# Row maximum before the rotary work in the first two steps of a unit of the attention network

## The reference

```
q = l2norm(q) * qs;  k = l2norm(k) * ksc                    # 16 heads of 64
q = q * cos * scale + rotate_half(q) * sin * scale          # rotation; k the same with 1/scale
sim = einsum(q, k in a window) * 8, masked
attn = softmax(sim, -1);  out = attn @ v;  x = out @ Wo + x
x = (a * gelu(gate)) @ W2 + x                               # gated layer behind a layernorm
```

## Time and profile before

| | |
|---|---|
| three runs, median (lowest to highest) | 6375.76 us (6371.46 to 6377.16) |
| the profiled execution: its time | 6374.81 us |
| its span, first to last instruction | 6373.0 us |
| mean granted TensorE clock, share of full speed | 0.931 |
| busy: TensorE, VectorE, ScalarE, GpSimd | 87%, 66%, 59%, 41% |

### The profile page before, as it was taken

The page is one execution under the profiler, slowest core; times in us unless marked ns, Lnnn a source line. Parts: engine busy times, 40 slices in busy tenths (PEclk is TensorE's granted clock), DMA queues, the critical chain, the costliest instruction groups (busy, mean ns, idle before and its releaser), DMA issues. The chain is left out here.

```text
span 6373.0 us, 104346 instructions
## 1 busy us (share of the span) xinstructions
PE 5519.4 (87%) x31072; PEld 3054.5 (48%) x31072; DVE 4211.3 (66%) x6918; ACT 3758.3 (59%) x11805; POOL 2607.4 (41%) x2014
## 2 busy tenths in 40 slices
PE   6888877777768999899998999899998999899997
PEld 3333333223225555555555555555555555555553
DVE  5666665333337777777777777777777777777775
ACT  3444443232226767667766776667666667667775
POOL 2122211000005555555554555555555555555553
PEclk9989988677679999999999999999999999999998
DMA  1000000000012222222222222222222222222222
GB/s 39 0 0 0 0 0 20 0 0 0 0 50 54 48 47 52 52 51 48 48 57 51 48 47 49 53 55 48 49 51 52 51 48 48 57 52 48 49 47 67
DMA packets 160228, 244.68 MB, mean 38 GB/s; under 512 B 51280, under 2 KB 51280, under 8 KB 158928
## 3 DMA queue, kind: packets, MB, share of 16 engines
q1 hardware_dynamic: 159696, 238.34, 15.2%
HBM read 30.52 MB, written 6.29 MB: 6 GB/s over the span
## 5 line engine op out<-in xcount | busy, mean ns | idle before, releaser
L323 POOL TENSOR_TENSOR c_Pb<-c_Pb,c_rs 96x512 f32<-96x512 f32 (+1 forms) x960 | 998.2, 1040 | 1459.4 <-DVE c_rs L715 1459.3
L385 ACT ACTIVATE c_Pb<-c_S,c_nb 96x128 f32<-96x128 f32 (+1 forms) x3840 | 1348.1, 359 | 159.9 <-DVE c_nb L706 158.5
L722 DVE COPY c_PTs<-c_S 128x384 f32<-128x384 f32 (+1 forms) x960 | 558.4, 582 | 623.9 <-PE c_S L506 622.8
L706 DVE TENSOR_REDUCE c_nb<-c_S 96x4 f32<-96x512 f32 (+1 forms) x960 | 657.1, 684 | 401.0 <-PE c_S L496 400.8
L335 POOL TENSOR_TENSOR c_rot<-c_tAB 128x1024 f32<-128x1024 f32 x384 | 910.1, 2370 | 0.8 <-DVE c_tAB L685 0.8
L396 ACT ACTIVATE c_OT<-c_PO 128x192 f32<-128x192 f32 (+1 forms) x960 | 324.4, 338 | 767.9 <-PE c_PO L520 767.4
L385 ACT ACTIVATION_READ_ACCUMULATOR c_Pb<-c_S,c_nb 96x1 f32 (+1 forms) x3840 | 757.7, 197 | 0.0
L329 POOL TENSOR_TENSOR c_sqs<-c_sq 128x512 f32<-128x512 f32 x384 | 488.0, 1271 | 610.4 <-ACT c_sq L363 610.4
L496 PE MATMUL c_S<-c_QK 64*96 64x128 f32 (+1 forms) x7680 | 666.4, 292 | 0.0
L506 PEld LDWEIGHTS c_S<-c,c_Pb 96*128 96x128 f32 (+1 forms) x3840 | 434.0, 142 | 368.0 <-issue 212.5
L520 PE MATMUL c_PO<-c_PTs,c_V 128*64 128x96 f32 (+1 forms) x7680 | 555.8, 266 | 20.1 <-issue 19.5
(11 more groups left out here) (267 smaller groups left out, 10879.5 us busy)
## 6 DMA issues: line engine op xcount, KB each, us to landing
c_QK<-c_F SPq DMA_DIRECT2D x3072, 64.0 KB, 2.0
c_stage<-in_w_heads SPq DMA_DIRECT2D x36, 256.0 KB, 3.0
a_W<-in_w_level SPq DMA_DIRECT2D x1, 3335.5 KB, 11.0
c_WT<-in_w_tails SPq DMA_DIRECT2D x6, 537.5 KB, 5.4
b_W<-in_w_level SPq DMA_DIRECT2D x1, 3133.0 KB, 10.0
c_WT<-in_w_tails SPq DMA_DIRECT2D x6, 512.0 KB, 4.2
x<-in_x SPq DMA_DIRECT2D x1, 2048.0 KB, 7.5
x_kept<-x SPq DMA_DIRECT2D x1, 2048.0 KB, 6.3
```

What stands on the lines that cost most here:

```text
L323: nc.gpsimd.tensor_tensor(p, p, r, ALU.mult).then_inc(*p_ready.up())
L385: e = nc.scalar.activation(Pb[0:m, n % 3, i, :], S[0:m, 2 * (n % 2) + r, c * SPAN_K:(c + 1) * SPAN_K], ACT.Exp, bias=nb[0:m, n % 2, i:i + ...
L706: nc.vector.tensor_reduce(nb[0:m, n % 2].rearrange("p (b c) -> p b c", b=2), S[0:m, b:b + 2, 0:2 * SPAN_K].rearrange("p b (c k) -> p b c k ...
L722: nc.vector.tensor_copy(PTs[:, n % 2].rearrange("p (b c) q -> p b c q", b=2)[:, :, :, 0:m], S[:, b:b + 2, 2 * SPAN_K:].rearrange("p b (c q ...
```

## The change

In VectorE's `step`, four lines move from ahead of `row_max` to behind it. In steps with t = 0, `finish` of the q job now comes behind the row maximum, and in steps with t = 1, `products` of half 1 of the k job does. Nothing is added or removed, and the other engines' lists are the same.

```
@@ VectorE's step
-                    if t == 0 and tk:
-                        finish(jk - 1, tk)
-                    if t == 1 and tk:
-                        products(jk, 1, tk)
                     if n == 2 and now:
                         v_copy(1, 0, PA, now)
...
                     if now:
                         row_max(n, now)
+                    if t == 0 and tk:
+                        finish(jk - 1, tk)
+                    if t == 1 and tk:
+                        products(jk, 1, tk)
                     if t == 0 and tk:
                         products(jk, 0, tk)
```

## The result

| | before | changed |
|---|---|---|
| runs of this comparison, median (lowest to highest) | 6373.86 us (6371.46 to 6377.16), 4 runs | 6538.38 us (6524.08 to 6539.84), 4 runs |
| the profiled execution: time, span | 6374.81, 6373.0 us | 6524.08, 6522.3 us |

The change makes the kernel slower by 2.5%: the ratio is 1.0250, with a 95% interval from 1.0235 to 1.0264. The forecast was 6562, in a range from 6495 to 6620. The profiled execution is the shortest of the four; the other three lie at 6537 to 6540.

The account below looks back on a forecast made before the run. TensorE was taken as the bound, waiting for `finish`: 2.97 us per turn times 48 turns gives 143 us, plus 43 us for clock falls, on 6374.8 us: 6561, or 6562 against the median, range 6495 to 6620.

Parts of the forecast that it names:

- Step 0: First t = 0 step: the projection waiting for `finish` starts 0.65 us later, 0.85 together with step 2's 0.2.
- the 0.2 of step 2: In step 2 the later `products` lets TensorE's projection start at 3943.92 instead of 3943.73, 0.2 us later.
- Step 5: At t = 0 the projection starts 1.38 us later, waiting for `finish`; 0.43 is absorbed, leaving 0.95.
- the 0.1 of step 7: In step 7 the later `products` costs 0.1 us, by the same sum as in step 2.
- moves by the same 1.38: Behind step 5's projection on TensorE, the transpose, copy of probabilities and scores of step 6 each move by 1.38 us.
- Step 10: At t = 0 the projection moves from 3980.18 to 3981.68, by 1.50 us; 0.43 is absorbed, leaving 1.07.
- Step 15: The gated layer's matmuls stand ahead of the projection on TensorE, so the later `finish` costs nothing.
- the gaps and what surrounds them are nearest to those of step 13: New gaps in steps 5 and 10 bring clock falls at step 13's share, 20/42: 43 us for 96 gaps.
- Rival 1: The dependency costs as forecast, but TensorE's clock does not fall in the new gaps: 6518 us, chance 0.26.
- Rival 4: The row maximum is on the chain setting the end; 0.6 us earlier shortens each unit: 115 us faster, 6260, chance 0.05.
- the gain side is empty: Exponentials of steps 5 and 15 start 0.3 and 0.6 us earlier, but TensorE's following work queues behind the projection: no gain.
- Rival 2: The clock falls nearly each time in the new gaps and the delays of `rotate` show: 6609 us, chance 0.08.

Follow-up runs that it names:

- t0_only: Kernel before, with only `finish` (t = 0) moved behind the row maximum and `products` left ahead: 6503.03 us against 6376.35, ratio 1.0199.
- half_finish: Changed kernel, with `finish` computing only 256 of the 512 tokens: 6445.04 us against 6377.4 for the kernel before, ratio 1.0107.
- last_unit_only: Kernel before, with both moves made only in steps 15 and 16: 6386.31 us against 6376.35, ratio 1.0017.
- t1_only: Kernel before, with only `products` of half 1 (t = 1) moved behind the row maximum: 6356.8 us against 6376.35, ratio 0.9967.
- late_proj: Changed kernel, with TensorE's projection of half 1 moved to just ahead of the next step's scores: 6517.62 us, ratio 1.0222 to the kernel before.
- before_split_first: Kernel before, with the weight split ahead of `products` of half 1 in steps 1, 6, 16 of layer-change turns: 6353.58 us against 6377.12, ratio 0.9963.
- after_split_first: Changed kernel, with the weight split ahead of `products` of half 1 in steps 1, 6, 16 of layer-change turns: 6500.65 us, 1.0195 of the kernel before.
- step11_only: Kernel before, with `products` of half 1 behind the row maximum only in step 11, not in layer-change turns: 6335.15 us against 6377.12, ratio 0.9936.
- both_gains: Kernel before, with step 11's `products` behind the row maximum and the weight split first in layer-change turns: 6320.28 us against 6377.4, ratio 0.9911.
- fill_gap: Changed kernel, with TensorE computing the values of steps 3 and 8 three times: 6513.55 us against 6377.12 for the kernel before, ratio 1.0221.

## Why the prediction was right, and where its terms were off

**The mechanism: right.** TensorE's projection waits for `finish`, 1.44 us in steps 5 and 10 as worked out, 0.39 in step 0 (worked out: projection at 3938.99, where the gap comes to 0.38), and nothing in step 15. `t0_only` alone gives the turn of 91.6 us, and `half_finish` moves the wait with the length of `finish`. The idle time ahead of L472 is absorbed as said.

**The ordinary turn: 2.97 forecast, 2.5 measured.** The shifts of the row maxima within a turn show where the difference is. Step 0: 0.85 forecast, 0.65 measured; the 0.2 of step 2 found idle time of the scores behind it, which waited for the copy anyway. Step 5: 1.05 forecast with the 0.1 of step 7, about 0.75 measured; the step that failed is "moves by the same 1.38". Before, the copy of the probabilities was queued on VectorE behind `products` until 3959.99, so scores of step 6 had a delay of their own which the new one covers. Now the copy waits 0.25 us for the transpose. Of the 0.3 this is 0.18: from the start of the projection to that of the mask of step 6 it is 3960.59 - 3958.40 = 2.19 us before and 3937.84 - 3935.83 = 2.01 now.

```profile
3960.59 0.42 PE L491 MATMUL c_S<-c 128*96 128x256 bf16 x2
```

From there to the sum of squares it is 3962.54 - 3960.59 = 1.95 us before and 3939.24 - 3937.84 = 1.40 now, so 0.55 is absorbed there, and not 0.43. Step 10: 1.07 forecast, 1.0 measured. Step 15: nothing in both; the 0.6 gained by its row maximum is given back in the next step, as `last_unit_only` shows.

**The other turns: mis-sized.** The sum multiplied by 48, as if all turns were alike, and cost the move of `products` at 0.2 and 0.1. In the layer-change turns TensorE's waits for the copy grow too (by 2.1 us in the turn looked at above), and these turns cost 7.1 each, of which up to 2.6 is the clock, by TensorE's longer busy time. The first and the last turn cost 6.7 each. That the sum came near is in part luck, since ordinary turns cost less than forecast and the seven others more: the forecast was 143 for waits, and the measured growth without the clock is 149 less some 13, so 136 (an estimate, from the next paragraph).

**The clock: over-sized.** Forecast 43 us, from 20 falls in 42 gaps of 1.47 us applied to 96 new gaps. In the changed kernel's trace 11 of 98 gaps of 1.44 us are followed by a fall, and of the 42 of step 13 only 9 still are: 20 falls again. In the network TensorE's clock stood at 1.2 GHz for 335 us before and for 366 us changed. At half the clock 31 us more cost at most 15; the busy time of the layer-change turns alone gives 13, so I take some 13 us for the profiled execution. The other three runs, at a granted clock of 0.928 and not 0.931, took 13 to 16 us longer, so by the median it is some 27 of the 164.5 us. Both are estimates. Ordinary turns have hardly any part in it: their falls are no more than before (58 us at 1.2 GHz in 41 of them, 78 before). One of the 11, from a layer-change turn: the first matmul behind it takes 0.80 us where 0.50 is usual, and the second 0.63 where 0.40 is.

```profile
4124.59 0.80 PE L465 MATMUL c_PA<-c_xh,c_WH 128*128 128x512 f32 x1 [1.44 <-DVE c_F L696]
4125.19 0.63 PE L466 MATMUL c_PA<-c_xh,c_WL 128*128 128x512 f32 x1
```

The step that failed is "the gaps and what surrounds them are nearest to those of step 13": the length is the same, the share of falls is not. The rule of the Trainium skill that the prediction weighed (TensorE: Matmul & The Clock Gate, section on HAM oscillation) names only much longer gaps as harmful. Going by it alone the clock would stay up; the rows above show a fall, so this trace does not agree.

**The rivals.** Rival 1, no falls, 6518, is as near as the forecast: the median lies between them, 20 above the one and 24 below the other. Rival 4, that the row maximum is on the chain that sets the end, holds at one place, step 11, for 0.45 us a turn; "the gain side is empty" was wrong there. I had asked only what follows on TensorE, and the path goes over ScalarE's list into step 13. The reason given, "ScalarE is not the bound", looked at the whole turn; from step 11 to 13 ScalarE has hardly a pause. In the changed kernel the gain is absent, since there the late scores hold the row maximum of step 11 (the rows under `t1_only`). Rival 2's delay of `rotate` on the normalisation did not show in ordinary turns.

## What to carry to other kernels

Before an instruction is moved behind a wait, look for the first instruction of the bounding engine that needs its result, and at how much slack stands there: here `finish` of step 5 had none, ending with the values of TensorE at 3958.34, and an earlier row maximum paid at one of the places tried. Read the turns of every kind: the late `products` gained 0.4 us in an ordinary turn and lost 3.2 in each of 5. When a loss has been found, moving the waiting instruction along is no remedy by itself; `late_proj` shows the wait again at the next edge of the cycle.

## What the hardware showed that I had not expected

A subtraction on VectorE from SBUF to SBUF (L773, 128x512) takes 0.69 us alone. If a GpSimd tensor_tensor has started ahead of it, it ends about 0.55 us behind the end of that one, however long that takes: beside `rotate` (above) at 4131.28 + 2.72 = 4134.00, where `rotate` ends at 4130.99 + 2.46 = 4133.45, and so in all 15 such places of the kernel before and the 15 of the changed one (0.54 to 0.56). Beside the shorter `normalise`, in `before_split_first`, it takes 1.41:

```profile
4020.28 1.22 POOL L323 TENSOR_TENSOR c_Pb<-c_Pb,c_rs 128x512 f32<-128x512 f32 x1
...
4020.64 1.41 DVE L773 TENSOR_TENSOR c_WL<-c_stage,c_WH 128x512 fp32r<-128x512 f32 x1
```

where 4022.05 is again 0.55 behind 4021.50. So VectorE's instruction as good as waits for GpSimd's to end; it is not merely slowed. Where it starts first (five places there, 0.09 us ahead of GpSimd's sum of squares) it keeps its 0.69 us, and the sum takes 1.73 us in place of 1.27. With the order changed so that they do not meet, all 36 take under 0.70:

```profile
L773 DVE TENSOR_TENSOR c_WL<-c_stage,c_WH x36: 691/693/694, 1889.8 to 5694.8; 128x512 fp32r<-128x512 f32 x36
```

(shortest, median and longest in ns, `after_split_first`; in the changed kernel the longest is 2733). The row maximum and the copy of the probabilities, which read PSUM, keep their 0.69 us when a `rotate` covers them whole, in 181 and 171 executions of the trace of before. What VectorE and GpSimd share there, no run here tested.

The share of equal gaps behind which TensorE's clock falls is not a constant of the gap: for the 1.47 us of step 13 it was 20 of 42 before, 9 in the changed kernel, 6 in `t1_only`, 3 in `step11_only`, 1 in `both_gains`, 18 in `fill_gap`, 21 and 22 in `t0_only` and `last_unit_only`, and 28 in `half_finish`. The order around it differs by tenths of a microsecond. What decides it stays open.
